# Which engine subtracts which piece of the moved probabilities, and when, in a grouped attention on one Trainium2 core

## The reference

```python
q = q * cos + _rotate_half(q) * sin
k = k * cos + _rotate_half(k) * sin
qg = q.reshape(b, NKV, GROUPS, s, HD)
scores = jnp.einsum('bkgqd,bksd->bkgqs', qg, k) / jnp.sqrt(jnp.asarray(HD, dtype))
scores = jnp.where(causal[None, None, None], scores, -inf)
attn = jax.nn.softmax(scores.astype(jnp.float32), axis=-1).astype(dtype)
out = jnp.einsum('bkgqs,bksd->bkgqd', attn, v)
```

## Time and profile before

| | |
|---|---|
| time, median of 3 runs | 2245.55 us (2245.01 to 2254.09) |
| time of the profiled execution | 2250.93 us |
| its span, granted TensorE clock over it | 2249.1 us, 0.97 |
| PE busy | 2103.7 us, 94% |
| DVE busy | 1689.1 us, 75% |
| ACT busy | 1339.6 us, 60% |
| POOL busy | 1218.1 us, 54% |

### The profile page before, as it was taken

How to read it: one execution, slowest core, us unless ns; L and a number is a source line. 1 busy time by engine, 2 the same in 40 slices (tenths; PEclk the granted TensorE clock), 3 DMA queues, 4 the chain that set the end, 5 groups by cost and what they waited for, 6 DMA issues and landing times. The chain is left out here.

```text
span 2249.1 us, 37941 instructions
## 1 busy us (share of the span) xinstructions
PE 2103.7 (94%) x10343; PEld 1751.7 (78%) x10343; DVE 1689.1 (75%) x2940; ACT 1339.6 (60%) x3541; POOL 1218.1 (54%) x921
## 2 busy tenths in 40 slices
PE   6899899999899967999999999999999999968998
PEld 5777777777777756888888888888888888756887
DVE  6778878878778876878878878788788887884322
ACT  6767666666666635656656666566566665553321
POOL 3767777776767555645455454564454544453400
PEclk9999999999999988999999999999999999988999
DMA  2534334344333531444444443444444443442310
GB/s 81 141 94 115 105 87 119 98 108 112 89 105 93 159 96 41 104 119 106 102 117 111 115 110 102 106 115 115 110 109 100 115 115 93 121 120 86 102 51 24
DMA packets 165856, 231.19 MB, mean 103 GB/s; under 512 B 47280, under 2 KB 77136, under 8 KB 165744
## 3 DMA queue, kind: packets, MB, share of 16 engines
q1 hardware_dynamic: 165744, 229.97, 38.9%
HBM read 114.23 MB, written 6.55 MB: 54 GB/s over the span
## 5 line engine op out<-in xcount | busy, mean ns | idle before, releaser
L90 POOL TENSOR_TENSOR l_probsT_lo<-l_moved,l_probsT_hi 128x512 fp32r<-128x512 f32 x192 | 254.9, 1333 | 401.0 <-ACT l_probsT_hi L940 263.8
L934 ACT ACTIVATE l_probs<-l_score,l_negtop 128x512 f32<-128x512 f32 x256 | 175.9, 687 | 354.8 <-DVE l_negtop L1045 343.3
L90 DVE TENSOR_TENSOR l_probsT_lo<-l_moved,l_probsT_hi 128x512 fp32r<-128x512 f32 x224 | 308.8, 1379 | 32.3 <-ACT l_probsT_hi L940 32.1
L1842 ACT ACTIVATE l_probs<-l_score,l_negtop 128x128 f32<-128x128 f32 (+3 forms) x256 | 134.6, 526 | 220.4 <-DVE l_negtop L1957 219.6
L83 PE MATMUL l_score<-l_kT_lo,l_qT_hi 128*128 128x512 f32 (+3 forms) x512 | 194.0, 379 | 64.4 <-POOL l_qT_lo L90 40.0
L1045 DVE TENSOR_REDUCE l_negtop<-l_score 128x1 f32<-128x512 f32 x256 | 175.5, 686 | 75.3 <-PE l_score L85 72.7
L83 PE MATMUL l_out<-l_w_out_lo,l_oT_hi 128*128 128x512 f32 x512 | 207.5, 405 | 2.2 <-DVE l_oT_lo L90 1.5
L1957 DVE CUSTOM_DVE_ANT_0 l_score<-l_score,l_mask 128x128 f32<-128x128 f32 (+3 forms) x256 | 125.5, 490 | 104.3 <-PE l_score L85 104.1
L85 PE MATMUL l_out<-l_w_out_hi,l_oT_hi 128*128 128x512 f32 x512 | 202.5, 396 | 0.0
L84 PE MATMUL l_out<-l_w_out_hi,l_oT_lo 128*128 128x512 f32 x512 | 202.3, 395 | 0.0
L83 PE MATMUL l_general<-l_w_qk_lo,xT_hi 128*128 128x512 f32 x504 | 197.4, 392 | 2.4 <-PEq L1447 2.4
(11 more groups left out here) (249 smaller groups left out, 6326.5 us busy)
## 6 DMA issues: line engine op xcount, KB each, us to landing
l_moved<-l_blocks SPq DMA_DIRECT2D x1024, 64.0 KB, 2.0
l_moved<-l_blocks SPq DMA_DIRECT2D x512, 80.0 KB, 2.1
l_inv_all<-inv_rows SPq DMA_DIRECT2D x32, 512.0 KB, 4.2
l_raw_out<-l_wo SPq DMA_DIRECT2D x64, 256.0 KB, 3.8
l_inv_all<-inv_rows SPq DMA_DIRECT2D x64, 256.0 KB, 3.6
l_raw_q<-l_wq SPq DMA_DIRECT2D x32, 256.0 KB, 3.8
l_raw_qk<-l_wq SPq DMA_DIRECT2D x64, 128.0 KB, 2.9
l_raw_qk<-l_wk SPq DMA_DIRECT2D x64, 128.0 KB, 3.0
```

Of the source, the lines that this page charges most:

```text
L90: return engine.tensor_tensor(out, full, hi.bitcast(F32), ALU.subtract)
L934: act.activation(probs[:, n % NPR], score[n % 2][:], ACT.Exp, bias=negtop[:, n:n + 1], accum_out=total[:, n:n + 1]).then_inc(s_exp, 1)
L1842: act.activation(probs[:, n % NPR, 0:width[t]], score[n % 2][:, 0:width[t]], ACT.Exp, bias=negtop[:, n:n + 1], scale=-1.0, accum_out=total ...
```

## The change

It changes two tables and the waits of TensorE that go with them. Upper halves, on ScalarE: pieces 2 and 3 move from lag 20 to 19, piece 4 from 21 to 20. Lower halves, a step later each: piece 0 moves from POOL to DVE, in the same step as piece 1; piece 2 moves from DVE to POOL, and POOL makes 2 and 3 in the step at lag 20; DVE makes piece 4 at lag 21 instead of 22. Each engine has as many pieces as before. The first product with V now waits for DVE's first two pieces, and no longer for POOL.

```diff
-LAND0_AT = {18: (0, 1), 20: (2, 3), 21: (4,)}
-PIECES0, EVEN0, ODD0 = 5, (1, 2, 4), (0, 3)
+LAND0_AT = {18: (0, 1), 19: (2, 3), 20: (4,)}
+PIECES0, EVEN0, ODD0 = 5, (0, 1, 4), (2, 3)
...
-                    wait_past(pe, s_lo_even, m, len(EVEN0) * SLOTS // 2, len(EVEN0) * pair + (1, 3)[odd])
-                    wait_past(pe, s_lo_odd, m, len(ODD0) * SLOTS // 2, len(ODD0) * pair + (1, 2)[odd])
+                    wait_past(pe, s_lo_even, m, len(EVEN0) * SLOTS // 2, len(EVEN0) * pair + (2, 3)[odd])
+                    if odd:
+                        wait_past(pe, s_lo_odd, m, len(ODD0) * SLOTS // 2, len(ODD0) * (pair + 1))
```

## The result

| | before | after |
|---|---|---|
| median of 4 runs (each) | 2248.12 us (2245.01 to 2254.09) | 2221.33 us (2219.18 to 2221.99) |
| profiled execution, its span, granted clock | 2250.93, 2249.1 us, 0.97 | 2221.65, 2219.9 us, 0.98 |
| PE, DVE, ACT, POOL busy | 94, 75, 60, 54% | 94, 75, 60, 55% |

The ratio is 0.9876 (95% interval 0.9852 to 0.9900): 26.8 us, 1.2% faster. The direction is right and the size is not. (The median of before is here over four runs, 2.6 us above the 2245.55 that the prediction started from.)

The account below looks back on a forecast made before the run. TensorE sets the pace, its open time mostly waits for POOL's `qT_lo`. Terms -9.0 (step 8), -2.8 (clock), 0 (step 24), +3.1 (step 0), -1.0 (stage end) sum to -9.7 us: 2236 us from 2245.55, range 2225 to 2250.

Parts of the forecast that it names:

- the chain: From step 3 to step 8, POOL and DVE operations take turns on their shared port until `qT_lo`: 12.35 us.
- rival A: POOL's addition slips in before DVE's piece 0; piece 1's reader stops 1.07 us at step 5: 2260 us, chance 0.12.
- B: A trade only: step 8's chain meets later turns, its gain shrinks to 0.1 us or nothing: 2246 us, chance 0.22.
- The price of a turn: Net time per operation on the port that DVE and POOL share: POOL 1.25 us, DVE 0.60 us.
- Parts 1 and 2: New lower-half shares, and pieces 2 and 3 split a step sooner: `qT_lo` 1.29 us sooner at step 8, -9.0 us.
- the terms for steps 24 and 0: `qT_lo` at step 24: no gain, 0; at step 0: 0.44 us later, seven times, +3.1 us.
- The sign that the prediction named: TensorE's waits for `qT_lo` still sum to about 40 us; those for the exponential fall to about 8.
- The clock (-2.8 us): Behind step 8, half of four falls of TensorE's granted clock go, 1.4 us each: -2.8 us (0 to -5.6).
- The end of the stage (-1.0 us): TensorE's 1.95 us wait for piece 4 at 791.68, half counted as gained: -1.0 us (0 to -2).
- rival C: Clock up after all step 8 waits, one idle turn caught at step 24, no step 0 loss: 2226 us, chance 0.16.

Follow-up runs that it names:

- the exchange alone: Kernel before with only the new shares of lower halves between DVE and POOL, the second bank's pieces split at the old lags: 2264.59 us, ratio 1.0056.
- the weight early: Changed kernel with the first query weight of a group split two steps sooner: 2204.15 us, ratio 0.9788 to the kernel before.
- the split alone: Kernel before with only the upper halves at the new lags 18, 19, 20, lower halves by the old table: 2234.40 us, ratio 0.9918.

## Why the prediction was wrong

**Right.** TensorE's waits are at steps 8, 24 and 0. The turns come in the order of the chain, with POOL's multiply first and both DVE pieces straight behind the cosine. In the looped passes no bank's first product waits for a piece (in the first pass one does, 1.37 us at 78.76 us, and three in the last). So rival A did not occur. B is refuted too: `qT_lo` came 1.95 us sooner at step 8 and not 0.1, and the exchange pays once the split is early.

**The price of a turn (Parts 1 and 2, and the terms for steps 24 and 0).** The step that failed is the net price of 1.25 and 0.60 us. Queued turns cost 1.14 and 0.58, so each chain was forecast too long by 0.5 to 0.7 us (thirteen queued turns are 11.46 us; the first and the last of POOL's are not queued behind DVE and take 1.30 and 1.23, which makes 11.71):

| chain | forecast | measured |
|---|---|---|
| to step 8 | 12.35 us | 11.69 |
| to step 24 | 13.6 us | 13.09 |
| to step 0 | 10.5 us | 9.97 |

The last two go by POOL after, ahead of step 24 and of step 0, against the earlier trace rows:

```profile
347.33 1.30 POOL L2042 TENSOR_TENSOR l_rope<-l_rope,l_trig 128x512 f32<-128x512 f32 x1 [4.14 <-ACT l_rope L1800]
...
359.15 1.27 POOL L90 TENSOR_TENSOR l_qT_lo<-l_rope,l_qT_hi 128x512 fp32r<-128x512 f32 x1
...
372.99 1.31 POOL L2042 TENSOR_TENSOR l_rope<-l_rope,l_trig 128x512 f32<-128x512 f32 x1 [2.94 <-ACT l_rope L1800]
...
381.68 1.28 POOL L90 TENSOR_TENSOR l_qT_lo<-l_rope,l_qT_hi 128x512 fp32r<-128x512 f32 x1
```

Measured from the sine's multiply, `qT_lo` is sooner by 1.95 us at step 8 (forecast 1.29), by 0.57 at step 24 (forecast 0), and by 0.09 at step 0 (forecast 0.44 later). Seven times each: -13.7, -4.0 and -0.6 us in place of -9.0, 0 and +3.1. A long chain multiplies a small error: 0.1 us in a turn became 12.4 us in the sum. The sign that the prediction named went with it: the waits for `qT_lo` were to stay at about 40 us and are 25.8. (Of the seven stops at step 24 that the prediction counts as alike, the first pass's is 4.02 us.)

**The clock (-2.8 us).** I took 1.4 us for a fall, half of step 8's four gone, and none of step 24's. It is 1.6 us. Up to step 8 of the last pass the kernel before has three falls at step 8 and seven at step 24, of which two count double; the changed kernel has none at step 8 and six at step 24. 12 - 6 = 6 times 1.6 is -9.6 us. (The fourth fall at step 8 is behind that last step 8, and its gain is in the next term.) Both parts of the size were too small: the stop at step 8 became 0.94 us, not 1.4, and I had put the term for step 24 at nothing.

**The end of the stage (-1.0 us)** had the wrong sign. The wait of 1.95 us for piece 4 did go, and one of 4.98 us for DVE's pieces became 3.19 (at 773.44). But TensorE waits elsewhere for DVE: 0.96 and 0.27 us for its pieces, and 1.90 for `oT_lo` at 766.33. In all it waits 16.7 us behind step 8 of the last pass, before 16.4. From that step to the next stage's first turn of the rows it takes 124.94 us, before 123.8: +1.1 us.

The sum by these values is -13.7 - 4.0 - 0.6 - 9.6 + 1.1 = -26.8 us, where the medians differ by 26.8. That the two agree to 0.1 us is luck: the ratio's interval allows 22 to 33 us, and the sum goes by the profiled executions, which differ by 29.2 us in span. At the last step 8 TensorE is 28.5 us ahead (the sum has 27.9), and at the next stage's start 27.3; the other 1.9 us lie behind the stage, and no run here says what they are. That is the content of rival C (clock up, step 24 a little sooner, step 0 no worse), beyond its 2226 us and with a chance of only 0.16. As the rows at hand could not exclude any of its three parts, that was too little.

## What to carry to other kernels

Where two engines take turns at a port, take the price of a turn from the ends of operations that all stood in the queue, and count how often the chain uses it before you trust the sum. Look at which split or copy releases the queue before you exchange work in it: here the exchange alone was a loss, and with the earlier split it was a gain. Price a stop of TensorE with the clock that it costs: here cutting one stop in three, or filling it with products that nobody needs, saved a fall of 1.6 us each time, though what TensorE waited for came no sooner.

## What was not expected of the hardware

- A stop of 2.2 to 2.4 us at step 8 or 24 is followed by the granted clock's lower level in most cases (10 of 13 before, 6 of 7 after) and in some not; a stop of 0.9 us at step 8 in no case (0 of 7 after, 0 of the 10 read with the weight early). Stops of 0.39, 0.62 and 1.29 us with work between them had none behind them (0 of 6), though together they are 2.3 us, and those of 1.59 and 1.29 us in the split alone had none either (0 of 6). The length of one stop is not all that counts: in the last pass of the kernel before, stops of 0.89 and 0.80 us 2 us apart were followed by the lower level (0.82 in the window from 753.70 to 757.90).
- Products that compute nothing used made the kernel 17.8 us faster: 0.9921 (0.9904 to 0.9937).
- A subtraction of 128x256 with two SBUF operands took 0.68 us beside POOL, and held up the one behind it by a turn of POOL, 1.1 us. A transpose of the same size took 0.40 us and held up nothing that the chain shows.
